# Second expert layer of a four-layer network: tokens scattered into expert order instead of gathered by lists

## The reference

```python
    x = L0_attn_x
    x = _layernorm(x + _L0_attn_ref(...), axis=-1)
    x = _layernorm(x + _L0_ffn_ref(...), axis=-1)
    x = _layernorm(x + _L1_attn_ref(...), axis=-1)
    x = _layernorm(x + _L1_ffn_ref(...), axis=-1)

    def _L1_ffn_ref(x, ln1_w, ..., router_w, w1, w2):
        ...                                   # attention over the sequence: x1
        hn2 = layernorm(x1, ln2_w, ln2_b).reshape(s * b, h)
        logits = hn2 @ router_w.T
        rp = jax.nn.softmax(logits, axis=-1)
        topw, topi = jax.lax.top_k(rp, K)     # E, K, F = 8, 2, 256
        gates = jnp.sum(jax.nn.one_hot(topi, E, dtype=hn2.dtype) * topw[..., None], axis=1)
        hmid = jax.nn.gelu(jnp.einsum('th,ehf->tef', hn2, w1), approximate=False)
        y = jnp.einsum('tef,efh->th', hmid * gates[:, :, None], w2)
        return x1 + y.reshape(s, b, h)
```

## Time and profile before

| | |
|---|---|
| Runs | 2444.89, 2450.25, 2463.81 us (median 2450.25) |
| Profiled execution | 2455.95 us, span 2454.2 us |
| Busy share of the span | PE 78%, PEld 65%, DVE 62%, ACT 53%, POOL 43% |
| DMA | 353.95 MB in 198,092 packets |
| POOL, L1400 (row gathers, both expert layers) | x296, 281.1 us busy, 950 ns each |
| POOL, L1393 (result gathers, second expert layer) | x128, 122.0 us busy, 953 ns each |
| PE, L1449 (hidden layer, both expert layers) | x1184, 214.1 us busy, 310 ns each |

### The profile page before, as it was taken

One profiled execution on the slowest core, in us unless ns is written; L12 is line 12 of the kernel. 1 busy time (PEld: TensorE's weight loads), 2 busy tenths in 40 slices (PEclk: granted clock), 3 DMA queues, 4 the chain that ended last, 5 costly groups with the idle time before them and its releaser, 6 DMA issues. The chain is left out here.

```text
span 2454.2 us, 52714 instructions
## 1 busy us (share of the span) xinstructions
PE 1912.8 (78%) x16756; PEld 1586.3 (65%) x16788; DVE 1526.3 (62%) x6215; ACT 1288.9 (53%) x3105; POOL 1049.3 (43%) x1285
## 2 busy tenths in 40 slices
PE   7799999999897897888578988699998758756500
PEld 6555555555555896887467777588887657755400
DVE  2577878878886583421279997588887564313345
ACT  3688888888884322344358887344443104423310
POOL 2133333333331315555578885322222115566564
PEclk9899999999998898999889999899999559976755
DMA  7899999999995104555412221000001115543333
GB/s 242 279 315 312 310 309 315 315 312 312 313 313 162 61 1 119 150 155 155 116 30 63 59 61 43 17 1 1 1 1 35 69 37 150 153 120 109 98 79 74
DMA packets 198092, 353.95 MB, mean 144 GB/s; under 512 B 25280, under 2 KB 145856, under 8 KB 196800
## 3 DMA queue, kind: packets, MB, share of 16 engines
q1 hardware_dynamic: 140752, 294.77, 36.9%
q0 software_dynamic: 17664, 36.21, 6.2%
q10 hardware_dynamic: 39408, 19.60, 2.7%
HBM read 165.87 MB, written 145.52 MB: 127 GB/s over the span
## 5 line engine op out<-in xcount | busy, mean ns | idle before, releaser
L1400 POOL DMA_INDIRECT moe_route_rows_sb<-tokens,moe_taken x296 | 281.1, 950 | 285.8 <-PE moe_route_bank L1440 109.0
L179 POOL TENSOR_SCALAR_AFFINE_SELECT heads_raw_relative<-heads_raw_relative 128x508 f32<-128x508 f32 x256 | 166.9, 676 | 494.6 <-ACT heads_raw_relative L564 454.9
L1561 DVE COPY moe_route_y<-moe_route_bank 128x128 f32<-128x128 f32 x296 | 82.9, 289 | 415.6 <-PE moe_route_bank L1458 237.4
L1449 PE MATMUL moe_route_bank<-moe_route_rows_t,moe_route_w_now 128*128 128x128 f32 x1184 | 214.1, 310 | 90.1 <-ACT moe_route_rows_t L1500 51.0
L564 ACT COPY heads_raw_relative<-heads_rel_bank 128x768 f32<-128x768 f32 x247 | 199.0, 805 | 121.7 <-PE heads_rel_bank L459 121.3
L488 PE MATMUL attend_turn_bank<-ident,attend_score 128*128 128x128 f32 x1536 | 230.7, 286 | 21.3 <-ACT attend_prob_t L570 20.9
L1449 PEld LDWEIGHTS moe_route_bank<-moe_route_rows_t,moe_route_w_now 128*128 128x128 f32 x1184 | 179.9, 218 | 100.0 <-issue 98.7
L488 PEld LDWEIGHTS attend_turn_bank<-ident,attend_score 128*128 128x128 f32 x1536 | 163.1, 141 | 117.4 <-ACT attend_prob_t L570 68.9
L1500 ACT COPY moe_route_rows_t<-moe_route_bank 128x128 f32<-128x128 f32 x296 | 79.2, 268 | 286.0 <-PE moe_route_bank L1440 122.5
L570 ACT ACTIVATE attend_prob_t<-attend_turn_bank 128x384 f32<-128x384 f32 x512 | 225.2, 501 | 6.2 <-PE attend_turn_bank L488 6.2
L574 ACT ACTIVATE attend_score<-attend_score,attend_extreme 128x128 f32<-128x128 f32 x512 | 215.6, 421 | 9.0 <-DVE attend_extreme L621 8.7
(11 more groups left out here) (321 smaller groups left out, 5074.3 us busy)
## 6 DMA issues: line engine op xcount, KB each, us to landing
shear<-heads_raw_relative SPq DMA_DIRECT2D x128, 768.0 KB, 5.3
heads_relative<-shear SPq DMA_DIRECT2D x128, 768.0 KB, 6.5
moe_route_w_now<-moe_w SPq DMA_DIRECT2D x296, 129.0 KB
expert_out<-moe_route_y ACTq DMA_DIRECT2D x73, 256.0 KB
qk_heads<-heads_qk_out SPq DMA_DIRECT2D x32, 256.0 KB, 4.3
heads_qk<-qk_heads SPq DMA_DIRECT2D x128, 64.0 KB
tokens<-moe_z SPq DMA_DIRECT2D x8, 1024.0 KB, 4.1
moe_route_rows_sb<-tokens,moe_taken POOLq DMA_INDIRECT x296
```

The lines of the kernel that those rows point to most:

```text
L179: m = nc.gpsimd.affine_select(out=future, in_=future, compare_op=ALU.is_ge, fill=-BIG, base=1 - P, pattern=[[0, QUAD], [1, P - 1]], channe ...
L1400: nc.gpsimd.indirect_dma_start(rows_sb[:, s % TAKEN, :], None, c.tokens, bass.IndirectOffsetOnAxis(ex.taken[:, s // S, s % S:s % S + 1], 0 ...
L1449: mm = nc.tensor.matmul(hid_bank[u][:, k * P:(k + 1) * P], w1_now[r][:, k * P:(k + 1) * P], rows_t[s % DEEP][:, :], start=True, stop=True)
```

## The change

The second expert layer is split into four groups of 16 columns of tokens, eight batches each, with `S` = 39 tiles per group, 156 in all (the first expert layer keeps two groups and its lists). It no longer makes lists and no longer writes `tokens`. Instead POOL scatters each column of `ex.z` twice, once for each chosen expert, to its sorted places in a new DRAM array `sorted_rows`: 128 indirect DMAs, 32 per group, all ahead of the gathers of results. SP reads three tiles at a time from there, in order, when a group's 32 scatters have landed (`sent`). Places that no token takes must hold something finite, so SP clears `sorted_rows` during `attend_batches` with 40 DMAs of 256 KB. Stores hold three tiles instead of four, 52 in place of 36. A gather of results waits until its group's tiles are stored. `combine` stands at tiles 80, 85, ..., 155 (`FIRST` = 2 `S` + 2, `EVERY` = 5): 16 among the tiles, 16 after.

```diff
 def choose_experts(nc, c, ex, logit, shared):
-            dve.wait_ge(c.tokens_out[ex.name], 16 * 4)
-            for part in range(half // PART):
+            if ex.listed:
...
+                dve.wait_ge(c.tokens_out[ex.name], 16 * 4)
+                for part in range(group // PART):
...
-            for u in range(GROUPS):
-                s = nc.vector.tensor_copy(per_tile[:, u, :, :], tile_bank[u][:, 0:half * n].rearrange("p (j e) -> p j e", e=n))
+            for u in range(2):
+                for g in range(per * u, per * (u + 1)):
+                    at = (g - per * u) * group * n
+                    s = nc.vector.tensor_copy(per_tile[:, g, :, :],
+                                              tile_bank[u][:, at:at + group * n].rearrange("p (j e) -> p e j", e=n))
...
+def route_sorted(nc, c, ex, func, extra, out):
+    S, CH, RING, ROWS, GOT, HELD, DEEP = ex.group_steps, 3, 8, 4, 4, 8, 3
+    FIRST, EVERY = 2 * S + 2, 5
+    per_batch = BLK * TOPK
+    per_group = BPG * per_batch
+    batch_after = lambda s: (s - FIRST) // EVERY if s >= FIRST and (s - FIRST) % EVERY == 0 else None
...
+        @block.gpsimd
+        def _(pool):
+            def gather(q):
+                t, m = q // per_batch, q % per_batch
+                if q % per_group == 0:
+                    chunks = (q // per_group + 1) * S // CH
+                    for u in range(2):
+                        pool.wait_ge(rows_out[u], 16 * len(range(u, chunks, 2)))
+                if m == 0 and t >= GOT:
+                    pool.wait_ge(added, t - GOT + 1)
+                nc.gpsimd.indirect_dma_start(got[t % GOT][:, m, :], None, c.expert_out[0:(q // per_group + 1) * S * P, :],
+                                             bass.IndirectOffsetOnAxis(ex.slots[:, q:q + 1], 0)).then_inc(gathered[t % GOT], 16)
+
+            pool.wait_ge(c.cleared, 16 * (SLOT_TILES // 4))
+            for q in range(B * per_batch):
+                nc.gpsimd.indirect_dma_start(c.sorted_rows[0:STEPS * P, :], bass.IndirectOffsetOnAxis(ex.slots[:, q:q + 1], 0),
+                                             ex.z[:, q // TOPK, :], None).then_inc(sent[q // per_group], 16)
+            for q in range(B * per_batch):
+                gather(q)
+
+        @block.sync
+        def _(sp):
+            for s in range(STEPS):
+                if s % LOADED == 0:
+                    experts = experts_of(mybir.EngineType.SP, s)
+                if s % CH == 0:
+                    q = s // CH
+                    if s % S == 0:
+                        sp.wait_ge(sent[s // S], 16 * per_group)
+                    wait_past(sp, turned, CH * (q - ROWS + 1))
+                    sp.dma_start(rows_sb[:, q % ROWS, :, :], c.sorted_rows[s * P:(s + CH) * P, :].rearrange("(k p) d -> p k d", p=P)
+                                 ).then_inc(rows_in[q % ROWS], 16)
+                if s >= RING:
+                    sp.wait_ge(hid_made, s - RING + 1)
+                    sp.wait_ge(hid_ready, s - RING + 1)
+                sp.dma_start(w1_now[s % RING][:, :], flat(ex.w1[:, bass.ds(experts[s % LOADED], 1), :])).then_inc(w1_in[s % RING], 16)
...
+            for s in range(STEPS):
+                output(s)
+                if batch_after(s) is not None:
+                    combine(batch_after(s))
...
 def attend_batches(nc, c, groups, fixed):
+        @block.sync
+        def _(sp):
+            sp.wait_ge(zeros_set, 1)
+            for k in range(SLOT_TILES // CLEAR):
+                sp.dma_start(c.sorted_rows[k * CLEAR * P:(k + 1) * CLEAR * P, :].rearrange("(k p) d -> p k d", p=P), zeros[:, :, :]
+                             ).then_inc(c.cleared, 16)
+            sp.wait_ge(c.cleared, 16 * (SLOT_TILES // CLEAR))
...
-            route(nc, c, ex, None, ACT.Gelu, True, groups, out)
+            route_sorted(nc, c, ex, ACT.Gelu, groups, out)
```

More of the change, by code:

```diff
@@ L1078, in choose_experts @@
 def choose_experts(nc, c, ex, logit, shared):
-    n = ex.n
+    n, G = ex.n, ex.groups
+    lists = ("high_int", "high", "slot_all", "low") if ex.listed else ()
     names = ("peak", "centred", "total", "recip", "gate", "g0", "is0", "score0", "best0", "first0", "rest",
              "g1", "is1", "score1", "best1", "first1", "either", "per_tile", "scan", "count", "count_up", "count_int",
-             "full", "tiles", "until0", "until", "begin", "base", "gap", "gap_all", "earlier_tiles", "place", "placed0", "slot0",
-             "placed1", "slot1", "high_int", "high", "slot_all", "low", "gate_sum", "gate_eps", "gate_inv", "past", "expert", "last_expert")
+             "full", "tiles", *(["until0"] * (G - 1)), "until", "begin", *(["base0"] * (G - 2)), "base", "gap", "gap_all", "earlier_tiles", "place", "placed0", "slot0",
+             "placed1", "slot1", *lists, "gate_sum", "gate_eps", "gate_inv", "past", "expert", "last_expert")
     vec = Count(*names)
@@ L1098, in choose_experts @@
         either = sb("either", [P, NT, n], BF16)
-        per_tile, scan, ones = (sb(x, [P, GROUPS, n, NT // GROUPS]) for x in ("per_tile", "scan", "ones"))
+        per_tile, scan, ones = (sb(x, [P, G, n, NT // G]) for x in ("per_tile", "scan", "ones"))
         count, count_up, tiles, until, begin, gap = (
-            sb(x, [P, GROUPS, n]) for x in ("count", "count_up", "tiles", "until", "begin", "gap"))
-        count_int, full = sb("count_int", [P, GROUPS, n], I32), sb("full", [P, GROUPS, n], I32)
+            sb(x, [P, G, n]) for x in ("count", "count_up", "tiles", "until", "begin", "gap"))
+        count_int, full = sb("count_int", [P, G, n], I32), sb("full", [P, G, n], I32)
         place = sb("place", [P, NT, n])
@@ L1169, in _ @@
                 shared_experts(t)
-            for part in range(half // PART):
+            for part in range(group // PART if ex.listed else 0):
                 r = part % 2
@@ L1177, in _ @@
                     mm = nc.tensor.matmul(token_bank[:, 0:S], at_low[r][:, k, :], at_token[r][:, k, :],
-                                          start=part == 0 and k == 0, stop=part + 1 == half // PART and k == COLS - 1)
+                                          start=part == 0 and k == 0, stop=part + 1 == group // PART and k == COLS - 1)
                 mm.then_inc(inverted, 1)
@@ L1244, in _ @@
             did("tiles")
-            for u in range(GROUPS):
+            for u in range(G):
                 nc.vector.tensor_tensor_scan(until[:, u, :], ones[:, 0, 0, 0:n], tiles[:, u, :], 0.0, ALU.mult, ALU.add
@@ L1250, in _ @@
             did("begin")
-            nc.vector.tensor_scalar(begin[:, 1, :], begin[:, 1, :], float(ex.group_steps), None, ALU.add).then_inc(vector_did, 1)
+            for g in range(1, G):
+                nc.vector.tensor_scalar(begin[:, g, :], begin[:, g, :], float(g * ex.group_steps), None, ALU.add).then_inc(vector_did, 1)
             did("base")
-            nc.vector.tensor_tensor(gap[:, :, :], scan[:, :, :, half - 1], count[:, :, :], ALU.subtract).then_inc(vector_did, 1)
+            nc.vector.tensor_tensor(gap[:, :, :], scan[:, :, :, group - 1], count[:, :, :], ALU.subtract).then_inc(vector_did, 1)
             did("gap")
@@ L1286, in _ @@
[L1286 to L1301 removed]
+                dve.wait_ge(made, begun + 2 + k)
```

336 lines of the change are left out of this document (269 added, 67 removed).

## The result

The changed kernel took 2475.97 us (median of 6 runs, 2472.27 to 2479.63), the kernel before 2450.16 beside it. The ratio is 1.0084, 95% interval 1.0062 to 1.0105: 0.8% slower, where I had forecast 2379 and a range of 2325 to 2440. The profiled execution took 2473.5 us, its span is 2471.8.

What follows compares the result with a forecast made beforehand. POOL's queue of gathers was taken to set the pace from 2151 to 2339. Choice -26, lead +34, 156 tiles in 249 us where 142 took 314, tail -20: span 2377.4 plus 1.75, 2379 us; range 2325 to 2440.

Steps and rivals of the forecast that it cites:

- Tiles 1 to 80: First 80 tiles of the second expert layer, beside the scatters: 1.55 us each, 124 us, ending at 2156.4.
- Choice: Choice of experts, before the first indirect DMA: token list goes, small DVE operations added; -26 us, first indirect at 1981.0.
- lead: From the first scatter to the first tile-output copy: wait for group 0's 32 scatters; +34 us, first copy at 2032.4.
- last 76 tiles: Tiles 81 to 156, only result gathers left on POOL: 1.65 us each, 125 us, to 2281.8.
- tail: From the last copy to the end, 52 gathers left: 95.6 us in place of 115.3.
- Zeros: 40 writes of 256 KB from SP in the sequences' attention: cost nothing, 10 us if a wait shows.
- Clock: Sign to check in both tile stretches: clock over 0.9.
- A: Rival, last 76 tiles: sums among the tiles, not POOL's queue, make them slow; 2.85 us each, 2471; chance 0.11.
- C: Rival, scatters: each costs 2.5 us, so tiles wait for each group; end at 2487, break-even near 2.25; chance 0.09.
- D: Rival, all tiles: clock stays low or DMA engines cannot go on; 1.9 us a tile, 2426; chance 0.14.
- B: Rival, tiles at 1.25 us without list and hand-overs, DVE waits for first gathers; 2341; chance 0.11.

## Why the prediction was wrong

*The failed step is "Tiles 1 to 80".* I took 1.55 us a tile beside the scatters, between two rows of stretches in which POOL's gathers waited for the tiles, their ring being full. I priced what scatters cost POOL and the DMA engines, both rightly (1.27 us, share far under 1), and gave a stream without waits the pace of one with waits. The runs show in its place that on chips with late signals the tiles all but stand while scatters or gathers run without a pause. The step from the first copy to that of tile 81 took 221.9 us where I had 124, 98 too many. With 4.4 from ahead of it, and 2 and 6 less behind, that is the whole miss of 94.5 (2473.5 against 2379).

*The lag stood in my own rows.* Before, the output matmuls start at 2016.26 and last 1.06, yet the copy starts at 2024.74, 7.4 us behind their end, with DVE idle. From 2007.08 to 2021.9 POOL had issued twelve gathers without a wait. The trace has five PE signals arriving together between 2024.71 and 2024.91, up to 7.1 us late, in the one pause of POOL there, before its gather at 2025.05. I read the first of those gathers and wrote "and a copy follows". The sum then put that copy 6.4 us behind the first transpose (10 in the changed kernel), and the one stretch of before with the new kernel's pattern went unread. The earlier trace rows had a hint of it: DVE's copies stood 69.4 us behind a "remote" releaser.

*Choice, lead, last 76 tiles and tail* were right to 1.5, 3, 2 and 6 us, not all of it by merit. The choice began 3.7 us later than before and was 2.2 shorter than I had it. For the last 76 tiles I took 1.65 us from rows that held a mean lag of 0.66 without my knowing it; the stretch had 0.57. Without the lag they took 1.28. *Zeros* cost nothing that shows: from POOL's first copy to `batch_hn_blocks` to the choice pass 391.4 and 392.5 us in the two profiles of before, and 391.0 to 392.6 in the changed kernel and its variants. *Clock:* it is 0.51 where the tiles stand. That is a consequence: the low level alone makes a tile 1.9 us, not 25.

*Two prices of the Trainium skill.* A scatter lands in a median of 2.2 us, where I had taken 3.1 from a gather's first use. The fit of the Trainium skill ("DMA: Bandwidth & Descriptors", section "Anatomy of one DMA — SWDGE (gpsimd) path") gives an estimate of 2.15: here page and trace agree. The 52 gathers of the tail mean 970 ns beside DVE's sums, against 957 before. The Trainium skill ("SBUF — State Buffer", section "Who interferes with whom") has a DVE operation in a two-port mode and one of GpSimd shut each other out; here that was again not worth a term.

*The rivals.* A put the slow pace down to the sums; with them the last 76 tiles took 1.62 us, so it is wrong. Before's 2.85 came with POOL's full queue and a mean lag of 2.0. C had the right outcome, tiles standing beside the scatters, from a price of a scatter that is wrong (1.27 us, where it needs 2.25). D has the clock of the bad stretch and not its pace, 1.9 us against 25. B is what happens where the signals are not late: 2341 was worked out from a start at 1981; that chip starts at 1931, 50 us earlier, which makes 2291 of it, and 2283 was measured. The last copy came at 2196, where B with that start has 2194; its tail was 83 us and not 96.

*What stays open.* What in the chip, or in how a core is placed on it, makes PE's signals late; which engine's path is shared; and why three signals pass in 25 us. The ends of matmuls are modelled in the trace, so it cannot tell a late signal from a result that PE finished late. Shown was only that POOL's indirect DMAs bring it on, that it grows as they stand closer together, and that two of the six chips of the experiments had none of it. The kernel before was not profiled on a chip without the lag. Of the 131 to 150 us that it differs by between the two kinds of chip, the first expert layer's 50 were measured in the same code; that the rest has the same cause is an inference. Each chip was visited once, so that it is the chip, and not something else that changed with the visit, is inferred too.

## What to carry to other kernels

When work is moved off the tile loop into a queue that runs free, price the loop beside a stream that waits for nothing, not beside the old one that waited for the loop; look for the one stretch in which the old queue ran free. A pause at every fourth indirect DMA, here a wait for its own landing, turned 0.8% slower into 1.4% faster where signals come late. Where they do not, the kernel with pauses at every third and later sums was 0.8% slower, and the change without pauses 1.4% faster; how much of that the pauses cost was not separated. Compare versions on more than one chip before choosing: the change as it stands is 0.7 to 0.8% slower on one kind and 1.4% faster on the other.

## What the runs showed of the hardware

- Beside indirect DMAs that POOL issues 1.27 us apart, PE's semaphore updates came 13 to 16 us late in the mean (22.8 at most) on a chip with late signals, scatters or gathers alike, and with 96 memsets in their place 0.01. ACT's came on time. DVE's are late by up to 5.0 us in the tail of the changed kernel (mean near 0.5), when PE has nothing to send, and 0.01 there on the chip without late signals.
- It depends on the chip: the mean lag was 0.01 us beside scatters on two of six chips, one of them with the very same stream. Their medians of the kernel before are 2315 and 2319 us; on the other four 2452 to 2465.
- More pauses free the signals further and cost POOL more: at every second DMA the lag falls to 0.18 us, but the scatters then stand 2.17 us apart in place of 1.62.
